# A decoder layer on one core: fetches of packed queries and keys one step sooner, bias lifting in the opening, two shared-expert pieces ahead of the routed stage, and a new placing of the side work

## What is computed

```python
x = x + attn(layernorm(x))       # 16 heads of 16; softmax(q1 k1) - lam * softmax(q2 k2), times v;
                                 # RMS norm per head, subln_w, W_proj, b_proj
x = x + xattn(layernorm(x), ctx, ctx)   # Wq, Wk, Wv, softmax(q k / 8), Wf, exact gelu, + ctx
x = x + ffn(layernorm(x))        # shared SwiGLU expert (256 -> 1024 -> 256) for every token, plus
                                 # the top 2 of 16 routed SwiGLU experts (256 -> 256 -> 256)
```

## Time and profile before

| | |
|---|---|
| median of 3 runs | 610.67 us (608.52 to 612.61) |
| the profiled execution | 611.33 us, of which the span of the trace is 610.1 us |
| PE busy | 552.2 us (91% of the span) |
| DVE busy | 312.4 us (51%) |
| ACT busy | 258.4 us (42%) |
| POOL busy | 230.0 us (38%) |
| mean granted clock of TensorE | 0.952 of full speed |

### The profile page before, as it was taken

One profiled execution on the slowest core, in us unless ns is written; L12 is line 12 of the kernel. 1 busy time (PEld: TensorE's weight loads), 2 busy tenths in 40 slices (PEclk: granted clock), 3 DMA queues, 4 the chain that ended last, 5 costly groups with the idle time before them and its releaser, 6 DMA issues.

```text
span 610.1 us, 10860 instructions
## 1 busy us (share of the span) xinstructions
PE 552.2 (91%) x3780; PEld 376.9 (62%) x3780; DVE 312.4 (51%) x683; ACT 258.4 (42%) x414; POOL 230.0 (38%) x473
## 2 busy tenths in 40 slices
PE   7987979799879887799999989997999999998998
PEld 5543436345536444556676457456999999997447
DVE  5679685597786994664442653110222222222282
ACT  6324454464654644624431300101666666663110
POOL 2436565455744554422001004664244344334000
PEclk8999889799999978789999989999999999999899
DMA  7744365332322238940009906222232333331721
GB/s 247 213 145 125 107 209 158 106 106 83 97 75 71 46 135 82 272 126 0 1 15 352 322 1 189 87 79 95 64 95 87 98 95 89 96 94 62 286 90 49
DMA packets 62197, 72.46 MB, mean 119 GB/s; under 512 B 14816, under 2 KB 55264, under 8 KB 60608
## 3 DMA queue, kind: packets, MB, share of 16 engines
q1 hardware_dynamic: 58160, 60.59, 34.6%
q0 software_dynamic: 3792, 10.39, 4.9%
q10 hardware_dynamic: 192, 0.79, 0.6%
HBM read 45.32 MB, written 26.03 MB: 117 GB/s over the span
## 4 chain that ended last, share of the span: by engine, by line
PE 42%; issue 18%; DMA 12%; DVE 11%; POOL 10%; ACT 4%; SPq 1%; ACTq 1%; POOLq 0%; DVEq 0%
PE ps L603 13%; DMA x_slots<-XN,slot_i 7%; POOL y_rows L1604 7%; PE ps L614 5%; PE ps L432 3%; PE ps L368 3%; DMA pack_k<-qk_parts 3%; PE ps L531 3%; DVE nmax L862 3%; PE ps L512 2%; PE ps L399 2%; PE ps L420 2%; PE ps L497 2%; PE ps L381 1%; POOL goes_to L1598 1%
## 5 line engine op out<-in xcount | busy, mean ns | idle before, releaser
L862 DVE TENSOR_REDUCE nmax<-ps 128x8 f32<-128x1024 f32 x64 | 77.7, 1215 | 37.7 <-PE ps L399 37.3
L659 PE MATMUL ps<-xt,Wn 128*128 128x128 f32 x752 | 93.4, 278 | 0.0
L659 PEld LDWEIGHTS ps<-xt,Wn 128*128 128x128 f32 x752 | 89.3, 195 | 0.3 <-ACT xt L1426 0.2
L1328 ACT ACTIVATE prob<-ps 128x1024 f32<-128x1024 f32 x64 | 65.5, 1023 | 38.0 <-PE ps L420 38.0
L1604 POOL DMA_INDIRECT y_rows<-yo,goes_to x47 | 45.9, 976 | 83.9 <-DVE yo L1117 83.6
L1109 DVE TENSOR_TENSOR ht<-sa,ps 128x256 f32<-128x256 f32 x47 | 19.8, 420 | 105.6 <-PE ps L670 95.5
L603 PE MATMUL ps<-xT,W1s 128*128 128x512 f32 x128 | 64.4, 628 | 3.4 <-DVE yo L1117 1.9
L1419 ACT ACTIVATE sil<-ps 128x512 f32<-128x512 f32 x32 | 19.1, 597 | 109.7 <-PE ps L603 109.7
L1439 ACT ACTIVATE Wn<-W 128x1024 f32 x47 | 49.7, 1057 | 29.7 <-issue 29.7
L603 PE MATMUL ps<-xT,W2s 128*128 128x512 f32 x128 | 61.0, 599 | 0.0
L614 PE MATMUL ps<-W3s,hTs 128*128 128x256 f32 x256 | 56.5, 381 | 3.5 <-DVE hTs L1040 3.5
(11 more groups left out here) (184 smaller groups left out, 856.8 us busy)
## 6 DMA issues: line engine op xcount, KB each, us to landing
W<-in_L_ffn_routed_w_dram SPq DMA_DIRECT2D x12, 1024.0 KB, 11.7
pack_q<-qk_parts SPq DMA_DIRECT2D x48, 128.0 KB, 3.0
xg<-x_slots SPq DMA_DIRECT2D x47, 129.0 KB, 2.1
x_slots<-zero SPq DMA_DIRECT2D x11, 512.0 KB, 10.6
qk_parts<-part SPq DMA_DIRECT2D x21, 256.0 KB, 2.8
pack_k<-qk_parts SPq DMA_DIRECT2D x42, 128.0 KB, 3.1
yg<-y_rows SPq DMA_DIRECT2D x4, 1024.0 KB, 8.8
X<-in_x_dram SPq DMA_DIRECT2D x4, 512.0 KB, 7.0
```

Of the source, the lines that this page charges most:

```text
L659: r = t.matmul(ps[:, 2 + p, h * P:(h + 1) * P], Wn[:, n % 3, k, h * P:(h + 1) * P], xt[:, p, k, :], start=(k == 0), stop=(k == KT - 1))
L862: v.tensor_reduce(nmax[:, s % 4, a, :, :], ps[:, b:b + 2, :].rearrange("p m (h t) -> p m h t", h=4), AX_X, ALU.max, negate=True).then_inc( ...
L1328: a.activation(prob[:, n:n + 2, :], ps[:, 2:4, :], ACT.Exp, scale=HD ** -0.5).then_inc(exped, 1)
```

## The change

It has five parts. (1) Before the loop PE does a few more transposes of the identity while it waits for the first norm; SP issues one piece of unit 0, then the last store of chunk 0, then the rest; `lift_queries` runs on DVE in the opening instead of step 5; `qk(2, 0)` and `qk(2, 1)` come later in PE's list; six casts go from DVE to ACT. (2) In the first steps the turn of chunk 3 and `qk(3, i)` are one step later, the turn and product of the weights four to five steps sooner, W_proj is loaded in step 7 instead of 3. (3) SP issues the fetches of units 3 to 7 in the steps with s % 4 of 0, 1 and 2, ahead of the stores; the load of context chunk 1 is in step 10 instead of 9. (4) The pieces of steps 9 to 31 have new places. (5) Two `up` pieces of chunk 3 run before the routed stage, in banks 4 and 5, and `Wn` lies 4 KB higher; after the loop `project_values` of chunks 2 and 3 come earlier in PE's list.

```diff
+AHEAD = 2
-ROUTED_WITH_UP = (0, 0, 2, 2, 2, 3, 3, 2)
+ROUTED_WITH_UP = (0, 0, 0, 0, 2, 3, 4, 3)
-TURN_AT = (1, 1)
-QK_AT = ((2, 0), (3, 0), (4, 0), (5, 0))
+STATS3_AT, NORM3_AT = (0, 0), (1, 1)
+TURN_AT = (2, 1)
+QK_AT = ((3, 0), (4, 0), (5, 0), (6, 0))
-WP_AT, LIFT_AT = (7, 0), (5, 0)
-WF_AT, A_AT, B_AT, M_AT = (5, 1), (6, 1), (7, 0), (7, 1)
-CTX_AT = {0: (9, 1), 1: (11, 1), 2: (17, 0), 3: (24, 0)}
-KEYS_AT = {..., 3: ((24, 1), (25, 0))}
+WP_AT = (9, 1)
+WF_AT, A_AT, B_AT, M_AT = (1, 0), (1, 1), (7, 0), (7, 1)
+CTX_AT = {0: (9, 1), 1: (11, 1), 2: (17, 0), 3: (28, 0)}
+KEYS_AT = {..., 3: ((28, 1), (29, 0))}
-U_AT = {0: ((14, 1), (15, 0)), 1: ((21, 1), (22, 0))}
-OUT_AT = {0: ((13, 0), (13, 1)), 1: ((22, 1), (23, 0)), 2: ((29, 1), (30, 0))}
+U_AT = {0: ((14, 1), (15, 0)), 1: ((22, 1), (23, 0))}
+OUT_AT = {0: ((13, 0), (13, 1)), 1: ((21, 1), (22, 0)), 2: ((29, 1), (30, 0))}
+OUT_IN = {0: 6, 1: 6, 2: 0}
-ADD_AT = {0: (14, 0), 1: (23, 1), 2: (30, 1)}
-STATS_AT = {0: (14, 1), 1: (24, 0), 2: (31, 0)}
-NORMAL_AT = {0: (15, 1), 1: (25, 0)}
-ROWS_AT = {0: (17, 1), 1: (26, 0)}
-SCORES_AT = {0: (18, 0), 1: (26, 1)}
-FO_AT = {0: (20, 1), 1: (29, 0)}
-CTX_LOAD_AT = {0: 4, 1: 9, 2: 12, 3: 16}
+ADD_AT = {0: (14, 0), 1: (22, 1), 2: (30, 1)}
+STATS_AT = {0: (14, 1), 1: (23, 0), 2: (31, 0)}
+NORMAL_AT = {0: (15, 1), 1: (24, 0)}
+ROWS_AT = {0: (17, 1), 1: (24, 1)}
+SCORES_AT = {0: (18, 0), 1: (25, 0)}
+FO_AT = {0: (21, 0), 1: (27, 1)}
+CTX_LOAD_AT = {0: 4, 1: 10, 2: 12, 3: 16}
...
             for _ in range(WARM):
                 t.transpose(ps[:, 0, 0:P], ident[:, :], ident[:, :])
+            for ready in (norm.stated, norm.eps_added, norm.scaled):
+                t.wait_ge(ready, 1)
+                for _ in range(4):
+                    t.transpose(ps[:, 0, 0:P], ident[:, :], ident[:, :])
...
-            qk(2, 0)
             t.wait_ge(identb_made, 1)
+            t.wait_ge(norm.put, 2 * 3)
             turn_max(0)
             scores(2, 0)
-            qk(2, 1)
+            qk(2, 0)
             scores(2, 1)
             turn_max(1)
+            qk(2, 1)
...
+            for i in range(2):
+                project_values(2, i, 6 + i)
             t.wait_ge(o_turned, STEPS)
...
-            for i in range(2):
-                project_values(2, i, 6 + i)
             turn(norm, NC + 2, 4, xn)
             t.wait_ge(u_put, 2 * 2 + 1)
             cross_scores(2)
+            for i in range(2):
+                project_values(NC - 1, i, 2 + i)
             turn(norm3, 0, 4, rows(XN, 0))
             up(0, 0)
             route_logits(0)
...
             up(0, 1)
-            for i in range(2):
-                project_values(NC - 1, i, 2 + i)
             weigh_values(2)
...
             for j in range(CB):
                 down(2, j)
+            for f in range(AHEAD):
+                up(NC - 1, f)
...
-            for f in range(FS):
+            for f in range(AHEAD, FS):
                 up(NC - 1, f)
...
             sum_lambda()
+            lift_queries()
             split(1, 0)
...
-            split(1, 2)
-            split(1, 3)
+            subtract_first(1, 2)
+            subtract_first(1, 3)
...
-            fetch(0, range(PIECES - len(K_RUNS)))
+            fetch(0, range(1))
             store_half(1, 2)
+            fetch(0, range(1, len(Q_RUNS)))
+            fetch(1, range(PIECES))
+            store_part(1, 0)
             for s in range(LEAD - 1):
-                fetch(1, range(3 * s, 3 * s + 3))
-                if s == 0:
-                    store_part(1, 0)
                 put_max(s)
             store_part(1, 1)
             for s in range(STEPS):
                 if s + LEAD - 1 < STEPS:
                     put_max(s + LEAD - 1)
+                if s in (1, 2):
+                    fetch(2, range(3 * (s - 1), 3 * (s - 1) + 3))
+                if CB <= s and s // CB + UNITS - 1 < STEPS // CB and s % CB < 3:
+                    fetch(s // CB + UNITS - 1, range(2 * (s % CB), 2 * (s % CB) + 2))
                 if s == 0:
                     store_part(1, 2)
-                if s == 3:
+                if s in (3, 4):
+                    for i in ((0,), (1, 2))[s - 3]:
+                        store_part(2, i)
+                if s == 7:
                     for j in range(4):
...
-                if s in (1, 2):
-                    fetch(2, range(3 * (s - 1), 3 * (s - 1) + 3))
-                if CB <= s and s // CB + UNITS - 1 < STEPS // CB and s % CB:
-                    fetch(s // CB + UNITS - 1, range(2 * (s % CB) - 2, 2 * (s % CB)))
```

More of the change, by code:

```diff
@@ L156, in decoder_layer @@
         sub_row = small.put("sub_row", [P, VD])
+        spread = small.put("spread", [P, P // VD, VD])
         lam = small.put("lam", [P, 4, HD])
@@ L339, in scores_bank, with up_bank @@
             return n % 2 * 2 if n < 2 * LEAD else 0
+        def up_bank(c, f):
+            return 4 if c == NC - 1 and f < AHEAD else 0
         def xT_of(c):
@@ L567, in between @@
                         i = places.index((s, a))
-                        project_o(c, i, 6 + i)
+                        project_o(c, i, OUT_IN[c] + i)
                 for c in range(INSIDE):
@@ L847, in take_second @@
                 v.wait_ge(rests, 4 * c + i + 1)
-                if c == 2 and i == 0:
-                    for half in range(2):
-                        v.wait_ge(halves_stored[half], 16 * STORES)
                 v.tensor_copy(part[PART_OF[c]][:, 1, ORDER[i], :], rest[:, i % 2, :]).then_inc(seconds, 1)
@@ L967, in between @@
             def between(s, a):
-                if s == 0 and a == 0:
+                if (s, a - 1) in THIRD_CHUNK_AT:
+                    subtract_first(2, 2)
+                if (s - 1, a + 1) in THIRD_CHUNK_AT:
+                    subtract_first(2, 3)
+                if (s, a) == STATS3_AT:
                     stats(norm, 3, 3)
-                if s == 0 and a == 1:
-                    split(2, 2)
-                if s == 1 and a == 0:
-                    split(2, 3)
+                if (s, a) == NORM3_AT:
                     normalize(norm, 3, 3, xn)
@@ L978, in between @@
                     prepare_weights()
-                if (s, a) == LIFT_AT:
-                    lift_queries()
                 if (s, a) == M_AT:
@@ L992, in between @@
                     if (s, a) == ADD_AT[c]:
-                        add_o(c, 6)
+                        add_o(c, OUT_IN[c])
                     if (s, a) == STATS_AT[c]:
@@ L1240, in vector_program @@
                 add_shared(2, j)
+            for f in range(AHEAD):
+                gate_up(NC - 1, f)
             v.wait_ge(experts_known, 1)
@@ L1295, in put_second @@
                 a.wait_ge(rests, 4 * c + i + 1)
+                if c == 2 and i == 0:
+                    for half in range(2):
+                        a.wait_ge(halves_stored[half], 16 * STORES)
                 a.activation(part[PART_OF[c]][:, 1, ORDER[i], :], rest[:, i % 2, :], ACT.Copy).then_inc(seconds, 1)
@@ L1359, in between @@
                 if (s, a_) in THIRD_CHUNK_AT:
-                    put_first(2, 2 + THIRD_CHUNK_AT.index((s, a_)))
+                    i = THIRD_CHUNK_AT.index((s, a_))
+                    put_second(2, i)
+                    put_first(2, 2 + i)
+                if (s - 1, a_) in THIRD_CHUNK_AT:
+                    put_second(2, 2 + THIRD_CHUNK_AT.index((s - 1, a_)))
                 if (s, a_) == TURN_AT:
@@ L1418, in silu_up @@
                     a.wait_ge(gated, n - 1)
[L1419 removed]
+                a.activation(sil[:, f % 2, :], ps[:, up_bank(c, f), :], ACT.Silu).then_inc(silued, 1)
             def put_x(n):
@@ L1458, in scalar_program @@
             a.activation(lw[:, 2:4], lw[:, 0:2], ACT.Exp).then_inc(lam_exped, 1)
-            for i in range(2):
-                put_values(1, i)
+            put_second(1, 2)
+            put_values(1, 0)
+            put_second(1, 3)
+            put_values(1, 1)
             put_turned(norm, 2, 4, xT_of(2))
@@ L1512, in scalar_program @@
                 silu_up(2, f)
+            for f in range(AHEAD):
+                silu_up(NC - 1, f)
             a.wait_ge(experts_known, 1)
@@ L1824, in sync_program @@
                                  W_proj.rearrange("(a i j d) n -> i j d a n", i=2, j=4, d=VD)[i, j], head_weights_in)
-                if s == 4:
-                    for i in range(3):
-                        store_part(2, i)
                 if s == QK_AT[3][0] + 2:
```

73 lines of the change are left out of this document (38 added, 35 removed).

## The result

The changed kernel took 595.47 us, the median of 4 runs (595.04 to 595.60). The kernel before, run again beside it, took 609.95 (608.52 to 612.61). The ratio is 0.9756, interval 0.9721 to 0.9792. The profiled execution has a span of 594.4 us against 610.1, PE is busy for 541.0 us against 552.2, and the mean granted clock is 0.974 against 0.952, which is 2 x 0.026 x 594.4 = 31 us at half clock against 59.

A forecast was written before the change was run, and what follows sets the result against it. The prediction took PE to be the bound, idling in short waits with half clock behind most. Its terms summed to -16.7 us from the profiled 611.33, so 594.6, or 594.0 for the median; range 586 to 603.

The forecast's parts named there:

- Opening, -0.3: Until step 0: added transposes keep the clock up, -0.8; two more DMAs ahead of query pieces, +0.5; sum -0.3 us.
- Steps 1 to 6, -6: Loop steps 1 to 6: less DVE work and spread weight work shorten them from 39.3 to 33.3 us, -6.
- Step 9, -3.9: Step 9: fetching one step sooner removes the wait for keys, -2.2, and the half clock behind it, -1.7 us.
- Step 11, +5.2: Step 11: the later context load makes PE wait 3.5 us, with +1.7 of half clock; sum +5.2 us.
- Steps 12 to 22, -0.7: Steps 12 to 22: unit 6's wait and its clock go, -3.0; new waits of 1.2 and 1.1; sum -0.7 us.
- Steps 23 to 31, -3.5: Steps 23 to 31: spreading the same work saves a guessed quarter of 13.7 us idle and half clock, -3.5 us.
- After the loop, -2.8: After the loop: `project_values(3)` moves into PE's wait of 2.78 us, -2.8 us.
- Two ups ahead, -4.7: Routed stage and tail: two ups fill PE's wait, -4.0; DVE's row additions, +1.0; clock stays up, -1.7; sum -4.7 us.
- (a): Rival: the context lands in time and DVE is ahead in steps 21 and 22; 586.5 us, chance 0.17.
- (b): Rival: the first steps gain nothing, ACT taking DVE's place; 600.0 us, chance 0.17.
- (d): Rival: the opening's added transposes don't raise the clock; 594.8 us, counted within the forecast's 0.50, of which 0.35.
- (e): Rival on the slower side: half clock holds through steps 23 to 31; 620 us, chance 0.03.

The follow-up runs named there:

- e4: The changed kernel with SP's old opening order (unit 0's query pieces ahead of the last store, unit 1's fetches in two halves): 595.54 us, ratio 0.9785.
- b1: The kernel before with only the lift of the queries moved from step 5 into the opening: 607.64 us, ratio 0.9947.
- e3: The changed kernel with `put_fo(0)` back in (20, 1) and the U pieces of chunk 1 half a step later: 591.86 us, ratio 0.9742.

## Why the prediction was right, and where its steps were not

The time, 594.0 forecast and 595.47 measured, is right in good part by luck: steps 12 to 22 came out 6.3 us slower than forecast and the stretch after the loop 5.8 us faster, and nothing ties the two together. Point by point:

**Bounded by short waits and the half clock behind them**: borne out in sum. Of the 15.7 us of the span PE's idle time gives 4.5 (57.9 to 53.4 us). PE's busy time, with the same products and twelve more transposes, gives 11.2, and with the same work that is the clock: 28 us less of it are at half.

**Opening, -0.3**: +1.7 in the first profile and, in the repeat, +0.5. The term of -0.8 for the transposes was wrong: `qk` took 7.11 us as it said, but a quick or a slow `qk` made no difference to the start of step 0. The Trainium skill's rule (TensorE: Matmul & The Clock Gate, Part 4: PE-mode transpose), by which transposes don't raise the clock, named the outcome of the edit, nothing gained. The traces don't bear out its reason. From 2.70 to 7.10 us PE had nothing but transposes in the kernel before, the granted clock was 1.00, and their pace nearly doubled on the way: 4 of them fall in the half microsecond from 2.60, 8 in that from 5.10. What raised the pace is not shown. And the edit lost nothing because the clock was up without the added ones. Step 0 had no term; it is 1.2 us shorter (5.5 us in all profiles of the new order, 6.7 in the three of the kernel before and its edits), of which SP's order is 0.7 by `e4`.

**Steps 1 to 6, -6**: -7.0. The size is right. The lift by itself explains 2 to 3 us of it, and steps 3 to 5 are 4.8 to 5.4 us as foreseen. That step 6 "waits for little" was misread: it had the 1.66 us for the maxima that are shown with `b1`. In the changed kernel step 6 isn't: 6.6 us, for the maxima that the prediction had let come "up to 1 us late" as a bound. They were 1.3 us late (2.20 less the 0.92 that ACT holds PE anyway) and took the clock with them, +1.5 in steps 7 and 8. A bound had been given to the delay and none to what follows it.

**Step 9, -3.9**: -4.6, with the cause of the wait missed. "The last pieces of a unit are issued about 6 us sooner, and the wait of 2.72 us goes": that the sooner fetch was needed for it is true of units 6 and 7 alone: 1.74 and 0.91 us return when it is undone. In step 9 none returns, and moving the stores behind the fetch removes the wait by itself. The order of the queue was in the trace, and the prediction looked at the fetch's step only.

**Step 11, +5.2**: +5.8, the wait 4.63 us for 3.5, the turn behind it at half clock as said. Undoing it gave 3.1 us in that step and 4 to 6 in the median. SP's queue was 1.0 us later than added up, for the two stores that the sum left out, and the landing took 4.1 us and not 3.8.

**Steps 12 to 22, -0.7**: the mis-sized term. In eight profiles of kernels with the changed tables and the two new waits in them, this stretch took 69.6 to 73.1 us, mean 71.1; in three of the kernel before and its edits, 67.1 to 68.3, mean 67.8. That is +3.4: step 21 -0.2, step 22 +1.6, step 12 +1.0 behind the context's wait, steps 16 to 18 +0.9. The waits that were foreseen (1.2 us for `fo`, 1.1 for `X`) measured 1.35 and 1.19. Wrong was the -3.0 for unit 6: step 21, without its wait for keys, is 7.7 to 9.5 us, where the three had 8.0 to 9.2, since `fo` and the maxima hold it, and what half clock cost before it costs again.

**Steps 23 to 31, -3.5**: -3.8, nearly all of it clock (1.00 for 0.90). It is -2.7 and -2.8 against the two edits of the kernel before (49.1 and 49.2 us, clock 0.93). A quarter of idle and half clock was a guess, as the prediction says, and no run took the new places apart.

**After the loop, -2.8**: -8.6, the other mis-sized term. The move itself is worth 5.9 by its own undoing: the wait of 2.8 filled, the half clock on the ups behind it, 1.7, and smaller waits. The prediction had counted half clock behind the waits in the loop and behind that of the routed stage, and none behind this one. Most of the remaining 2.7 us is the clock at the loop's end: `project_values(2)` took 6.03 us before and 3.72 after. It took 3.72 in both edits of the kernel before as well, so this part is a matter of that execution; their stretch is 160.1 us, and against them the change is worth 7 to 9 us.

**Two ups ahead, -4.7**: -5.1 in the profile; undoing them cost 4.0 us by the medians and 5.9 by the ratios. Start, routed stage and tail came out within 0.2 us each, the last gate 0.8 us later than before.

Of the rivals, (a) is out, since the context waited in every kernel that loaded it in step 10; (b) and (c) are out by the profile; (d) fits the edit in its time, not in its reason. (e) is not only out but points the wrong way: the thin halves kept their clock.

## What to carry to other kernels

In an in-order DMA queue the block ahead of the transfer matters before its step does: two swapped blocks did here what moving three fetches by a step was credited with, while the sooner fetches, four DMAs more ahead of `put_max(7)`, made that small transfer late. Count a wait on the engine that bounds as the wait and, separately, as the work behind it at half clock, after the loop as well as in it; and add up the queue of each step for everything that shares it, since one item too many can cost more than its issue. A stage that looks 3 us better in one profile is not yet better.

## What the runs showed of the hardware

The same wait at the same place leaves PE at either clock. The wait of 1.35 us for `fo` in step 21 is in nine profiles of the changed kernel and its edits; the 8 products behind it took 1.97 us in four of them and 3.46 to 3.75 us in five. Two executions of the same code so differ by up to 3.3 us in a stage (14.3 and 17.6 in steps 6 and 7), and two sets of runs of it by 1.9 us in the median (595.47 and 593.61).

At a DMA share of 0.93 (80.50 to 87.06) the context's 512 KB took 5.3 us to land in the view of DMA issues, against 3.8 in the earlier trace rows:

```profile
Cx<-in_ctx_dram SPq DMA_DIRECT2D x1, 512.0 KB, 5.3
```

Whether the single gains add up is not shown, only that they may. Against the two medians of the changed kernel (593.61 and 595.47) the later context load gave 4.3 to 6.2 us when undone, the first context load moved back 2.7 to 4.6, the places of steps 20 to 23 1.8 to 3.6: 8.8 to 14.4 together. But `e3` can't be told from the changed kernel by its ratio, and the intervals of the other two touch that of the changed kernel. The version with most of it (the late fetches in place of the first context load, and `put_fo(0)` left where it was) gave 11.7 to 13.6, clear of the noise, and the time at half clock fell from 31 us to 10.
